# A feed-forward down product on one core: from a plain tiled product to a 2 by 2 Strassen block product

## The chip, the cores and the metric

The kernel runs on one core of one Trainium2 chip, as one program. The metric is the device time of one execution, in microseconds (us); lower is better. It is written engine by engine: TensorE (PE, the matrix products), VectorE (DVE), ScalarE (ACT) and GpSimd (POOL) each have their own list of instructions, SyncE (SP) issues all DMAs, and the lists meet only at counting semaphores. Each engine works its list in order: an instruction that waits holds up all behind it.

## The reference

Two decoder layers on x (2 x 512 x 1024). The change is in the last piece, the feed-forward of the second layer with low-rank (rank 16) additions to its weights:

```python
def _matmul_lora(x, w, a, b, scale=1.0):
    out = jnp.einsum('bsd,hd->bsh', x, w)
    out = out + jnp.einsum('bsr,hr->bsh', jnp.einsum('bsd,rd->bsr', x, a), b) * scale
    return out
gate = _matmul_lora(x, gate_w, gate_a, gate_b)
up = _matmul_lora(x, up_w, up_a, up_b)
hidden = jax.nn.silu(gate) * up                           # 1024 x 2752
out = _matmul_lora(hidden, down_w, down_a, down_b)        # 1024 x 1024
```

and the layer's output is x + out.

## The kernel before

Every large product is made of float16 pairs: an operand is split into a high part and a low part (value minus high part), and three matmuls of 128 x 128 weights by 512 columns (high x high, high x low, low x high) stand for one product. Making a pair takes ACT (the high part, a copy) and then DVE (the low part, a subtraction).

**Up and gate, "the slabs".** HID = 2752 hidden units are 21 slabs of 128 (j = 0 to 20) and a tail of 64 (TAIL = 21). For each slab, gate and up together are a 2 by 2 block product after Strassen: seven products of 12 matmuls in place of eight. The weight blocks are named A11, A12, S1, S2, S4, S3, A22; `form` (line 1674) makes the sums S1 to S4 on DVE, `block_hi` (987) and `block_lo` (1688) split them into a ring of 12 blocks. Low-rank parts are folded into the weights first: PE makes a rank-16 product (`fold`, 2462), and DVE adds it to the loaded weights (`slab_add`, 1666). What the products give is put together by DVE in `gate_second` (1700, waits for product S4), `up_second` (1706, waits for S3; product A22 of the same slab waits for it), `hidden_second` (1711), `hidden_first` (1717) and `hidden_rest` (1723), which leave the slab's hidden values as a pair in HIDT. The order of DVE's work is written out by hand at the end of the vector program, that of PE in `products` (92). SP loads a gate and an up slab of 512 KB per j (line 547), each as soon as the staging buffer of the one two slabs earlier is free.

**Down.** For each of 8 tiles of 128 output features (m) and both halves b of the 1024 rows, `down` (2554) sums over the 22 hidden tiles: 21 x 3 + 2 matmuls of 512 columns (the tail of 64 needs two), 65 x 16 = 1040 in all. The weights of the next m come in four pieces: `down_fold` (2542), `down_add` (1752), `down_hi` (1052), `down_lo` (1762), while PE works on the current m; their 1024 or 640 columns lie in two PSUM buffers in turn, and the outputs of m and m + 1 in two others. `finish` (1783) adds the scaled sum to the residual, which `residual_hi`, `residual_lo`, a transposing DMA (line 584) and `residual_sum` (1774) have brought in transposed form while the first m are worked on; `send` (503) writes it out. A hidden tile is used straight from HIDT.

Of the kernel before, what the change touches and what calls it, by code (L numbers as in the profile page):

```python
# [52 lines left out]
N_LOADS = N_DOWN + KD * NP  # L53
ZEROED = 8 + N_DOWN - N_DF
# [37 lines left out]
def products(j):  # L92
# [7 lines left out]
         + [(TAIL, "L3"), (TAIL, "L4")])  # L100
# [45 lines left out]
def build(nc, x, ctx, ctx_t, consts, small_w, w_branch, wq, wk, bqk, gate_w, up_w, tail_w,  # L146
          down_w, down_tail, gate_a, gate_bt, up_a, up_bt, down_a, down_bt, out_t, x_keep):
    stack = ExitStack()
    with stack:
# [50 lines left out]
        DWN = [SLAB[:, at * KB:at * KB + 2 * HT * P].rearrange("p (s k c) -> p s k c", s=2, k=HT) for at in (0, 13)]  # L200
        XR = XT[:, :, :, :, :].rearrange("p b s k t -> p (b s k t)").rearrange("p (g s d) -> p g s d", g=NT, s=2)
# [5 lines left out]
        XD = X[:, :, :].rearrange("p g d -> p (g d)").bitcast(F16).rearrange("p (s m t) -> p s m t", m=KD, s=2)  # L207
# [54 lines left out]
        DA, DB = LORA[:, D:D + HID], LORA[:, 0:D]  # L262
# [8 lines left out]
        def factors_of(g, si, sj):  # L271
# [26 lines left out]
        out_done, spilled, xd_ok = [sem("out_even"), sem("out_odd")], sem("spilled"), sem("xd_ok")  # L298
# [14 lines left out]
        fac_ok, s_add, comb, b_lo, d_add, d_lo, xr_lo, out_v = (  # L313
            sem(n) for n in ("fac_ok", "s_add", "comb", "b_lo", "d_add", "d_lo", "xr_lo", "out_v"))
# [11 lines left out]
        b_hi, sg_ok, hid_hi, p1_ok, p5_ok, p6_ok, d_hi, xr_hi = (  # L326
            sem(n) for n in ("b_hi", "sg_ok", "hid_hi", "p1_ok", "p5_ok", "p6_ok", "d_hi", "xr_hi"))
# [8 lines left out]
        fold_p, mul_p, dfold_p, down_p = (sem(n) for n in ("fold_p", "mul_p", "dfold_p", "down_p"))  # L336
# [17 lines left out]
            + [(("fold", n), s_add, n + 1) for n in range(BT, NS)]  # L354
            + [(("dfold", m, i), d_add, m * NP + i + 1) for m in range(KD) for i in range(NP)]))

# [81 lines left out]
        def block_source(j, name):  # L438


            st = [STAGE[(N_SLAB + 2 * j + i) % SLOTS].rearrange("p (h k c) -> p h k c", h=2, k=KD // 2)
                  for i in range(2)]
            a11, a12, a21, a22 = (st[i][:, h] for i in range(2) for h in range(2))
            if j == TAIL:
                return {"K1": (a11, 0, None, NS), "K2": (a12, 1, None, NS)}[name]
            s1 = ST[:, :].rearrange("p (k c) -> p k c", k=KD // 2)
            return {"A11": (a11, 0, None, 2 * j + 1), "A12": (a12, 1, None, 2 * j + 1), "A22": (a22, 1, None, 2 * j + 2),
                    "A21": (a21, 0, None, 2 * j + 2), "S1": (s1, 0, 1, 4 * j + 1), "S2": (s1, 0, 1, 4 * j + 2),
                    "S4": (a12, 0, 1, 4 * j + 3), "S3": (a21, 0, 1, 4 * j + 4)}[name]

        def down_pair(m):
            return PAIR[m % 2]
# [4 lines left out]
        def _(e):  # L457
# [45 lines left out]
            def send(m):  # L503
                for h in range(B):
                    hs = slice(h * HALF, (h + 1) * HALF)
                    e.wait_ge(out_v, B * m + h + 1)
                    e.dma_start(out_t[m * P:(m + 1) * P, hs], OUT[:, m % 2, hs]).then_inc(out_done[m % 2], 16)
# [31 lines left out]
            for n in range(NS):  # L539
# [4 lines left out]
                j, w_ = n // 2, up_w if n % 2 else gate_w  # L544
                at = N_SLAB + n
# [10 lines left out]
                elif n == SLOTS + 1:  # L556
                    for t in range(2):
                        for group in range(3):
                            turn_pieces(t, group)
                    for group in range(3):  # L560
                        for t in range(2, BT):
                            turn_pieces(t, group)
            factor(N_DF, down_bt)
            factor(N_DF + 1, down_a)
            for m in range(KD):
                for i, (k0, k1) in enumerate(PIECES):
                    at, p_ = N_DOWN + m * NP + i, m * NP + i
                    if p_ < SLOTS:
                        e.wait_ge(fac_ok, 8 + 4 + p_ - SLOTS + 1)
                    else:  # L570
                        e.wait_ge(d_lo, p_ - SLOTS + 1)
                    kp = HTAIL if k1 == HT else P
                    st = STAGE[at % SLOTS][0:kp, 0:(k1 - k0) * P].rearrange("p (k c) -> p k c", k=k1 - k0)
                    e.dma_start(st, down_tail[m] if k1 == HT else down_w[m][:, k0:k1, :]).then_inc(
                        stg_in[at % SLOTS], 16)
                if m == 0:
                    e.wait_ge(mul_p, len(ORDER))
                    e.wait_ge(spilled, 16 * BT)
                    for g in range(BT):
                        e.dma_start(X[:, g, :], x_keep[g * P:(g + 1) * P, :]).then_inc(x_in[g], 16)  # L580
                if m in (1, 2):
                    e.wait_ge(xr_lo, NT)
                    for g in range((m - 1) * BT, m * BT):
                        e.dma_start_transpose(XD.rearrange("p s m t -> p (s m) t")[:, :, g * P:(g + 1) * P],
                                              XR[:, g, :, :].rearrange("p s d -> p (s d)")).then_inc(x_in[g], 16)
                if m >= 2:
                    send(m - 2)
            send(KD - 2)
            send(KD - 1)
            for n in range(2):  # L590
                e.wait_ge(out_done[n], 16 * B * KD // 2)

        @prog.gpsimd
        def _(e):
# [130 lines left out]
            for b_, used in ((1, DONE[TAIL - 1, "S2"]), (0, len(ORDER))):  # L725
                e.wait_ge(mul_p, used)
                e.wait_ge(zero_ok, ZEROED + 1 - b_)
                e.memset(DWN[b_][P - HTAIL:P, 1, TAIL, :], 0.0).then_inc(zero_ok, 1)

        @prog.scalar  # L730
        def _(e):
# [255 lines left out]
            def block_hi(j, name):  # L987

                q = ready(j, name) - 1
                src, half, made, value = block_source(j, name)  # L990
                e.wait_ge(s_add if made is None else comb, value)
                if q < RING:
                    e.wait_ge(sc_p, NT)
                else:
                    e.wait_ge(mul_p, DONE[(q - RING) // NB, BLOCKS[(q - RING) % NB]])
# [38 lines left out]
            def tail_gate(b):  # L1034
# [16 lines left out]

            def down_hi(m, i):
                k0, k1 = PIECES[i]
                p_, kp = m * NP + i, HTAIL if k1 == HT else P
                at = N_DOWN + p_
                st = STAGE[at % SLOTS][0:kp, 0:(k1 - k0) * P].rearrange("p (k c) -> p k c", k=k1 - k0)
                e.wait_ge(d_add, p_ + 1)
                if m == 0:
                    e.wait_ge(mul_p, DONE[TAIL - 1, "S2"])
                elif m == 1:  # L1060
                    e.wait_ge(mul_p, len(ORDER))
                else:
                    e.wait_ge(down_p, 2 * (m - 1))
                last = e.activation(DWN[(m + 1) % 2][0:kp, 0, k0:k1, :], st, ACT.Copy)  # L1064
                if k1 == HT:
                    last = e.activation(DWN[(m + 1) % 2][P - kp:P, 0, k0:k1, :], st, ACT.Copy)
                last.then_inc(d_hi, 1)

            def residual_hi(g):
                e.wait_ge(mul_p, len(ORDER))  # L1070
                if g < BT:
                    e.wait_ge(x_in[g], TURNED + 16)
                else:
                    e.wait_ge(x3_ok, g + 1)
                e.activation(XR[:, g, 0, :], X[:, g, :], ACT.Copy).then_inc(xr_hi, 1)

# [217 lines left out]
            for j in range(TAIL):  # L1294
# [1502 lines left out]
```

## Time and profile before

| what | value |
|---|---|
| median of 3 runs | 1168.9 us (1167.17 to 1169.38) |
| the profiled execution, its own time | 1169.75 us |
| its span in the profile | 1167.9 us |
| PE busy, share of the span | 1103.2 us, 94% |
| DVE busy | 797.3 us, 68% |
| ACT busy | 484.6 us, 41% |
| slabs in the trace (products of j = 0 to 20 and the tail) | about 503 to 929 us |
| down product in the trace | 929 to 1165 us |

All times below are read from the profiled execution, in us from the start of its span; its own time is 0.85 us above the median. The start time of a matmul row says when it began; matmuls are pipelined, so the next may begin before the one before has ended. L numbers are lines of the kernel.

### The profile page before, as it was taken

How to read it: one execution, taken by the hardware profiler on the slowest of the kernel's cores; microseconds unless marked ns; L12 is line 12 of the kernel's file. 1: busy time of each engine (PE TensorE's matmuls, PEld its weight loads, DVE VectorE, ACT ScalarE, POOL GpSimd, SP SyncE). 2: the span in 40 equal slices, each digit the busy share in tenths (PEclk: the TensorE clock that was granted, in tenths of full speed). 3: DMA queues.
4: the chain of work that ended last, by engine and by line, in shares of the span. 5: the costliest groups of instructions: out<-in, count | busy, mean ns of one | idle time of the engine just before them, and what ended most of it. 6: DMA issues, size and time to landing. Idle time of an engine off the chain costs nothing.

```text
span 1167.9 us, 16025 instructions
## 1 busy us (share of the span) xinstructions
PE 1103.2 (94%) x6144; PEld 540.9 (46%) x6150; DVE 797.3 (68%) x1600; ACT 484.6 (41%) x731; POOL 154.2 (13%) x184
## 2 busy tenths in 40 slices
PE   4786999899999999969999999999999999999998
PEld 2343554654445444424444444444444444444443
DVE  8999988889994177877767676767766664333330
ACT  6896652873145134744343434434343341111110
POOL 4883350073004010000000000000001000000000
PEclk9997999999999999999999999999999999999999
DMA  9620000223032029864111212020111375322200
GB/s 367 270 97 1 2 1 1 73 69 112 1 108 86 1 60 248 194 131 93 71 57 53 72 38 72 37 73 36 73 37 39 89 198 120 111 66 68 65 14 25
DMA packets 80061, 97.19 MB, mean 83 GB/s; under 512 B 57776, under 2 KB 58416, under 8 KB 79984
## 3 DMA queue, kind: packets, MB, share of 16 engines
q1 hardware_dynamic: 79984, 96.16, 27.0%
q8 instruction: 49, 0.80, 0.3%
q14 instruction: 28, 0.23, 0.1%
HBM read 76.22 MB, written 6.29 MB: 71 GB/s over the span
## 4 chain that ended last, share of the span: by engine, by line
PE 76%; DVE 18%; ACT 3%; issue 2%; DMA 1%; SPq 0%; DVEq 0%; ACTq 0%
PE PAIR L2518 32%; PE PAIR L2170 13%; PE PAIR L2171 12%; PE PAIR L2172 12%; DVE X L1558 2%; DVE PAIR L1510 2%; PE PAIR L2473 2%; DVE LORA L1509 1%; DVE LORA L1511 1%; DVE POOL L1384 1%; PE PAIR L2550 1%; DVE BST L1356 1%; DVE BST L1357 1%; DVE X L1427 1%; DVE XT L1421 1%
## 5 line engine op out<-in xcount | busy, mean ns | idle before, releaser
L2170 PE MATMUL PAIR<-POOL 128*128 128x512 f16 x672 | 255.8, 381 | 2.3 <-DVE POOL L1601 2.3
L2171 PE MATMUL PAIR<-POOL 128*128 128x512 f16 x672 | 255.8, 381 | 0.0
L2172 PE MATMUL PAIR<-POOL 128*128 128x512 f16 x672 | 255.7, 381 | 0.0
L2518 PE MATMUL PAIR<-XT,POOL 128*128 128x512 f16 x1008 | 230.2, 382 | 10.6 <-DMA XT<-POOL 6.9
L2518 PEld LDWEIGHTS PAIR<-XT,POOL 128*128 128x128 f16 x1008 | 98.2, 98 | 127.1 <-issue 14.0
L2518 PE MATMUL PAIR<-X,POOL 128*128 128x512 f16 x504 | 115.7, 379 | 0.4 <-DMA X<-POOL 0.4
L2172 PEld LDWEIGHTS PAIR<-POOL 128*128 128x128 f16 x672 | 65.8, 98 | 80.3 <-issue 1.4
L2170 PEld LDWEIGHTS PAIR<-POOL 128*128 128x128 f16 x672 | 65.6, 98 | 69.3 <-DVE POOL L1601 4.3
L2171 PEld LDWEIGHTS PAIR<-POOL 128*128 128x128 f16 x672 | 65.7, 98 | 65.5 <-issue 0.6
L1064 ACT ACTIVATE POOL<-STG 128x1024 f16<-128x1024 f32 (+2 forms) x32 | 25.3, 790 | 169.7 <-DVE STG L1759 169.7
L1759 DVE SCALAR_TENSOR_TENSOR STG<-STG,PAIR 128x1024 f32<-128x1024 f32 (+2 forms) x32 | 28.3, 884 | 89.8 <-PE PAIR L2550 86.7
L667 POOL MEMSET STG<- 96x1024 f32 (+1 forms) x12 | 11.0, 923 | 522.5 <-DVE POOL L1691 475.7
L2518 PEld LDWEIGHTS PAIR<-X,POOL 128*128 128x128 f16 x504 | 48.4, 98 | 55.9 <-issue 1.1
L1691 DVE TENSOR_TENSOR POOL<-STG,POOL 128x512 f16<-128x512 f32 x107 | 69.7, 684 | 0.7 <-ACT POOL L996 0.7
L996 ACT ACTIVATE POOL<-STG 128x512 f16<-128x512 f32 x107 | 62.0, 621 | 3.7 <-DVE STG L1671 3.6
L1704 DVE TENSOR_TENSOR POOL<-POOL,PAIR 128x512 f32<-128x512 f32 x21 | 14.4, 688 | 71.4 <-PE PAIR L2518 71.4
L996 ACT ACTIVATE POOL<-ST 128x512 f16<-128x512 f32 x42 | 26.3, 626 | 80.6 <-DVE ST L1686 80.6
L2518 PE MATMUL PAIR<-T4B,POOL 128*128 128x512 f16 x252 | 57.8, 379 | 1.2 <-issue 1.2
L1671 DVE SCALAR_TENSOR_TENSOR STG<-STG,PAIR 128x1024 f32<-128x1024 f32 x43 | 52.1, 1214 | 0.0
L1510 DVE RECIPROCAL PAIR<-LORA 128x16 f32<-128x16 f32 (+1 forms) x168 | 46.8, 279 | 5.8
L2170 PE MATMUL PAIR<-XT,POOL 128*128 128x512 f16 x128 | 48.5, 379 | 1.2 <-ACT XT L906 1.2
L2172 PE MATMUL PAIR<-XT,POOL 128*128 128x512 f16 x128 | 48.5, 379 | 0.0
(305 smaller groups left out, 1707.9 us busy)
## 6 DMA issues: line engine op xcount, KB each, us to landing
STG<-in_gate_w SPq DMA_DIRECT2D x21, 512.0 KB, 3.5
STG<-in_up_w SPq DMA_DIRECT2D x21, 512.0 KB, 4.3
STG<-in_ctx_t SPq DMA_DIRECT2D x16, 512.0 KB, 3.8
STG<-in_ctx SPq DMA_DIRECT2D x16, 512.0 KB, 4.2
STG<-in_down_w SPq DMA_DIRECT2D x16, 512.0 KB, 3.6
POOL<-in_ctx SPq DMA_DIRECT2D x12, 512.0 KB, 11.1
X<-in_x SPq DMA_DIRECT2D x8, 512.0 KB, 9.7
out_t<-T4B SPq DMA_DIRECT2D x16, 256.0 KB, 2.0
```

The lines of the kernel that those rows point to most:

```text
L996: e.activation(block(j, name)[:, 0, :, :], src, ACT.Copy).then_inc(b_hi, 1)
L1064: last = e.activation(DWN[(m + 1) % 2][0:kp, 0, k0:k1, :], st, ACT.Copy)
L1510: chain(e.reciprocal(rr, rs))
L1558: i = e.scalar_tensor_tensor(xs, H[:, g, sj * CST:(sj + 1) * CST], factors_of(g, si, sj), xs, ALU.mult, ALU.add)
L1671: e.scalar_tensor_tensor(st, st, WS, PAIR[aux.pair("fold", n)][:, :], ALU.mult, ALU.add).then_inc(s_add, 1)
L1691: e.tensor_tensor(blk[:, 1, :, :], block_source(j, name)[0], blk[:, 0, :, :], ALU.subtract).then_inc(b_lo, 1)
L1759: e.scalar_tensor_tensor(st, st, WS, PAIR[aux.pair("dfold", m, i)][0:kp, 0:w_], ALU.mult, ALU.add).then_inc(d_add, 1)
L2170: e.matmul(dst, l_hi, r_hi, start=first, stop=False)
L2171: e.matmul(dst, l_hi, r_lo, start=False, stop=False)
L2172: return e.matmul(dst, l_lo, r_hi, start=False, stop=last)
L2473: i = e.matmul(PAIR[pr][:, k * P + c0:k * P + c0 + w], fa[0:GRP * 32, k * P:(k + 1) * P], fb[0:GRP * 32, j * P:j * P + w], start=True, sto ...
L2518: i = e.matmul(dst, blk[:, a_, k, :], src[:, b_, k, :], start=(opens and k == 0 and n == 0), stop=(k == KD // 2 - 1 and n == 2), skip_grou ...
```

## The change

The down product becomes a 2 by 2 block product after Strassen, like gate and up: output tiles in pairs (p = 0 to 3), rows in two halves, hidden tiles in 11 pairs (22 tiles, the tail padded with zeros). Each p is worked in three sets of 4, 4 and 3 tile pairs ("chunks", 12 in all), and a chunk is seven products of 3 matmuls per tile pair: 12 x 4, 12 x 4 and 9 matmuls a product, 7 x 33 x 4 = 924 in all.

```python
SETS = ((0, 4), (4, 8), (8, HT // 2))
NSET = len(SETS)
CHUNKS = NSET * KD // 2
```

**PE.** Each of the seven products of a p has a PSUM bank of its own for all three chunks, and one half bank (`bank_f`) takes the low-rank products, four for each chunk. So a low-rank product waits until DVE has added the one before it, and the first chunk of the next p writes the banks that hold the results of the last:

```python
bank_d = {"A11": PAIR[2][:, 0:HALF], "A12": PAIR[2][:, HALF:D], "S1": PAIR[3][:, 0:HALF], "S2": PAIR[0][:, 0:HALF],
          "S4": PAIR[0][:, HALF:D], "S3": bank_c, "A22": bank_b}
bank_f = PAIR[3][:, HALF:D]

def down_fold(j, i):
    d = j - HT
    e.wait_ge(s_add, NS + 4 * d + i)
...
for j in range(HT, HT + CHUNKS):
    first = 3 if j == HT else 0
    for n, name in enumerate(BLOCKS):
        down_product(j, name)
        if j + 1 < HT + CHUNKS and first <= n < first + 4:
            down_fold(j + 1, n - first)
```

`down_product` waits for its weight block, and in the first chunk of p = 1 to 3 for the bank: A11 for `first_ok` of the p before, A12, S1, S2, S4, S3, A22 for 1, 4, 3, 5, 8 and 13 of its 13 steps `acc_v`. For p = 0 it waits for the hidden values and the differences read back from DRAM.

**DVE and ACT, down.** Per chunk DVE makes four sums `down_add` (each of half the columns of a staged tile), four `form` and seven `block_lo`; ACT makes seven `block_hi`. Behind the last chunk of a p (`evacuate`, 13 steps on DVE, one `first_product` on ACT) the seven products are put together with the residual:

```python
def evacuate(p):
    o11, o12, o21, o22 = (out_part(a_, b_) for a_ in range(2) for b_ in range(2))
    j, at = HT + NSET * p + NSET - 1, ACCS * p
...
    e.wait_ge(sum_v, 2 * p + 1)
    scaled(o11, "A12", o11)
    e.wait_ge(first_ok, p + 1)
    e.wait_ge(acc_v, at + 1)
    added(o11, o21)
...
    e.wait_ge(acc_v, at + 12)
    scaled(o21, "A22", o21)
...
for d in range(1, CHUNKS + 1):
    if d < CHUNKS:
        j = HT + d
        down_add(j, 0)
        down_add(j, 1)
        block_lo(j, "A11")
        down_add(j, 2)
        down_add(j, 3)
        form(j, "S1")
...
        for name in ("S2", "S4", "S3", "A22"):
            block_lo(j, name)
    if d % NSET == NSET - 1:
        residual_sum(d // NSET, 0)
        residual_sum(d // NSET, 1)
    elif d % NSET == 0:
        evacuate(d // NSET - 1)
```

**The input's differences.** For each pair of hidden tiles three differences of half rows are needed as pairs. They are made in the slab loop, for a pair (j - 1, j) of slabs: on DVE `turn_first` or `turn_last` (one operation each) behind `hidden_first`, `turn_middle` (two) behind `hidden_second` of an odd j, `turn_lo` (two ahead of `gate_second`, one ahead of `up_second` of an even j), and on ACT three `turn_hi`. Eight of the eleven sets go to DRAM (`park`, 768 KB each) and come back at the end of the slabs (`back_in`).

**The residual** is now split, transposed and kept in DRAM within the slab loop: eight times (j = 2, 3, 4, 5, 7, 9, 11, 13) a `residual_hi` on ACT, a `residual_lo` on DVE ahead of `gate_second`, a transposing DMA ahead of the gate slab's load, and writes:

```python
                j, w_ = n // 2, up_w if n % 2 else gate_w
+               if n % 2 == 0 and j - 2 in R_AT:
+                   turn_residual(R_AT[j - 2])
                at = N_SLAB + n
...
+               if n % 2 and j - 2 in R_AT:
+                   keep_residual(R_AT[j - 2])
+               if n % 2 and 4 <= j and j % 2 == 0 and j // 2 - 2 < PARKED:
+                   park(j // 2 - 2)
```

`turn_residual(i)` waits for the i-th `residual_lo`. In the down stage it is read back by `load_sum` (4 x 256 KB for each p), whose last two reads stand ahead of the next p's first weights on SP:

```python
for p in range(KD // 2):
    load_sum(p, 0)
    load_sum(p, 1)
    for d in range(NSET * p + 2, min(NSET * p + 5, CHUNKS)):
        load_down(2 * d)
        load_down(2 * d + 1)
        if d == NSET * p + 2:
            load_sum(p, 2)
            load_sum(p, 3)
    send(p)
```

`load_sum(p, 2)` and `(p, 3)` wait for the two `residual_sum` of p.

**DVE at the end of a p, in the new order** (L1978 is `down_add`, L1865 `form`, L1870 `block_lo`, L2001 and L2004 `evacuate`; the first rows end the blocks of chunk 3, the first of p = 1):

```order
L1865 TENSOR_TENSOR STG<-STG,ST 128x512
L1865 TENSOR_TENSOR STG<-STG 128x512
L1870 TENSOR_TENSOR POOL<-ST,POOL 128x512
L1870 TENSOR_TENSOR POOL<-STG,POOL 128x512 x3
L2001 SCALAR_TENSOR_TENSOR T4B<-PAIR,T4B 128x512
L2004 TENSOR_TENSOR T4B<-T4B 128x512
L2001 SCALAR_TENSOR_TENSOR T4B<-PAIR,T4B 128x512 x3
L2004 TENSOR_TENSOR T4B<-T4B 128x512
L2001 SCALAR_TENSOR_TENSOR T4B<-PAIR,T4B 128x512 x2
L2004 TENSOR_TENSOR T4B<-T4B,LORA 128x512 x4
L2001 SCALAR_TENSOR_TENSOR T4B<-PAIR,T4B 128x512
L1978 SCALAR_TENSOR_TENSOR STG<-STG,PAIR 128x512 x2
```

The 13 steps of `evacuate` (L2001 and L2004) stand between the blocks of chunk 3 and the first sum of chunk 4 (the last row). Before, the only operations of the end of an m were one `residual_sum` and two `finish`, and PE waited for them not in the next m, but in the one after it.

**PE at the same place, in the new order** (L2892 is `down_product`, L2826 `down_fold`; the rows are the last products of chunk 2 and the first three of chunk 3):

```order
L2892 MATMUL PAIR<-POOL 128x512 x9
L2892 MATMUL PAIR<-X,POOL 128x512 x15
L2892 MATMUL PAIR<-LORA,POOL 128x512 x3
L2892 MATMUL PAIR<-POOL 128x512 x12
L2826 MATMUL PAIR<-LORA 128x128 x4
L2892 MATMUL PAIR<-POOL 128x512 x12
L2826 MATMUL PAIR<-LORA 128x128 x4
L2892 MATMUL PAIR<-POOL 128x512 x12
```

The row before the last is the second low-rank product of chunk 4; it waits for the first `down_add` of chunk 4 on DVE, and all products behind it wait with it.

**SP in the slabs, in the new order** (L592 is the transposing DMA of the residual, L676 a slab's load, L598 and L603 the writes to DRAM; before, this list held the two loads of each slab alone):

```order
L592 DMA_TRANSPOSE POOL<-POOL 128x16x128
L676 DMA STG<-in_gate_w 128x1024
L676 DMA STG<-in_up_w 128x1024
L598 DMA xt_keep<-POOL 128x8x128 x2
L592 DMA_TRANSPOSE POOL<-POOL 128x16x128
L676 DMA STG<-in_gate_w 128x1024
```

The load of slab j + 2 has moved behind a transposition that waits for DVE's `residual_lo` of slab j, and it is DVE's `slab_add` later in the same slab that uses it.

## Rows read from the trace of the kernel before

**Rows 1.** The page: busy time of PE, share of the span.

```profile
PE 1103.2 (94%) x6144; PEld 540.9 (46%) x6150; DVE 797.3 (68%) x1600; ACT 484.6 (41%) x731; POOL 154.2 (13%) x184
```

**Rows 2.** Windows: stretch, PE, PEld, DVE, ACT, POOL busy, granted clock, DMA share, GB/s.

```profile
600.00:900.00 300.00, 300.00 (x1583) 143.49 (x1581) 209.40 (x315) 122.56 (x207) 2.79 (x3) 1.00 0.15 53
930.00:1164.00 234.00, 234.00 (x1196) 109.85 (x1195) 82.48 (x95) 34.56 (x48) 0.00 (x0) 1.00 0.31 87
```

**Rows 3.** Timeline of PE, one slab period: start, length, engine, line, operation.

```profile
714.24 2.75 PE L2518 MATMUL PAIR<-XT,POOL 128*128 128x512 f16 x12
716.83 0.61 PE L2473 MATMUL PAIR<-LORA 96*128 96x128 f16 x8
717.28 2.76 PE L2518 MATMUL PAIR<-X,POOL 128*128 128x512 f16 x12
...
730.68 2.75 PE L2518 MATMUL PAIR<-T4B,POOL 128*128 128x512 f16 x12
733.27 2.75 PE L2518 MATMUL PAIR<-XT,POOL 128*128 128x512 f16 x12
```

**Rows 4.** Timeline of DVE, the same period; in brackets idle before and its releaser.

```profile
714.61 0.69 DVE L1721 SCALAR_TENSOR_TENSOR PAIR<-PAIR,POOL 128x512 f32<-128x512 f32 x1
715.21 0.68 DVE L1686 TENSOR_TENSOR ST<-ST,STG 128x512 f32<-128x512 f32 x1
715.92 0.69 DVE L1686 TENSOR_TENSOR STG<-STG,ST 128x512 f32<-128x512 f32 x1
...
723.11 0.69 DVE L1704 TENSOR_TENSOR POOL<-POOL,PAIR 128x512 f32<-128x512 f32 x1 [3.49 <-PE PAIR L2518]
...
724.92 1.21 DVE L1671 SCALAR_TENSOR_TENSOR STG<-STG,PAIR 128x1024 f32<-128x1024 f32 x1
728.29 0.69 DVE L1709 TENSOR_TENSOR POOL<-POOL,PAIR 128x512 f32<-128x512 f32 x1 [2.16 <-PE PAIR L2518]
```

**Rows 5.** Timeline of ACT, the same period: a high part.

```profile
718.05 0.62 ACT L996 ACTIVATE POOL<-STG 128x512 f16<-128x512 f32 x1
```

**Rows 6.** Timeline of PE: the last wait of the slabs, the first matmul of down.

```profile
920.60 0.61 PE L2550 MATMUL PAIR<-LORA 96*128 96x128 f16 x8 [0.78 <-DVE LORA L1663]
...
929.27 0.38 PE L2170 MATMUL PAIR<-POOL 128*128 128x512 f16 x1
```

**Rows 7.** Timeline of DVE: the last `finish`.

```profile
1164.75 0.69 DVE L1789 SCALAR_TENSOR_TENSOR T4B<-PAIR,T4B 128x512 f32<-128x512 f32 x1 [13.27 <-PE PAIR L2575]
```

**Rows 8.** Timeline of DVE: eight residual differences of 1024 columns.

```profile
938.52 9.17 DVE L1772 TENSOR_TENSOR XT<-X,XT 128x1024 f16<-128x1024 f32 x8 [0.80 <-ACT XT L1075]
```

**Rows 9.** Timeline of SP: a transposing DMA; time to issue.

```profile
497.57 1.47 SPq L501 DMA_TRANSPOSE X<-POOL  x1
...
511.45 2.48 SPq L501 DMA_TRANSPOSE X<-POOL  x1
```

**Rows 10.** Line L547, all loads of slabs: issue to landing.

```profile
DMA to landing us min/median/max: 3.3/4.1/6.2
```

**Rows 11.** The same line, 485 to 500: two loads right behind four transposing DMAs.

```profile
DMA to landing us min/median/max: 4.6/4.7/4.9
```

**Rows 12.** Line L574, 985 to 995: weights behind two DMAs of 256 KB.

```profile
DMA to landing us min/median/max: 5.1/6.0/6.3
```

**Rows 13.** Timeline of PE: idle stretches in brackets, and matmuls behind them.

```profile
109.31 0.38 PE L2170 MATMUL PAIR<-XT 128*128 128x512 f16 x1 [2.26 <-DVE XT L1545]
...
110.71 0.62 PE L2171 MATMUL PAIR<-POOL 128*128 128x512 f16 x1
...
515.28 2.75 PE L2518 MATMUL PAIR<-XT,POOL 128*128 128x512 f16 x12 [3.74 <-DVE POOL L1698]
...
525.79 5.08 PE L2518 MATMUL PAIR<-XT,POOL 128*128 128x512 f16 x12 [6.87 <-DMA XT<-POOL]
```

**Rows 14.** Windows around them, columns as in group 2.

```profile
110.00:115.00 5.00, 5.00 (x40) 2.36 (x39) 4.52 (x14) 5.00 (x10) 2.14 (x3) 0.66 0.00 0
...
525.00:530.00 5.00, 4.21 (x10) 1.50 (x11) 4.87 (x9) 1.24 (x2) 0.00 (x0) 0.50 1.02 191
```

More of the change, by code:

```diff
@@ new lines, in load_sum @@
+            def load_sum(p, i):
+                a_, b_ = ((0, 0), (0, 1), (1, 1), (1, 0))[i]
+                if i >= 2:
+                    e.wait_ge(sum_v, 2 * p + i - 1)
+                elif p:
+                    e.wait_ge(acc_v, ACCS * (p - 1) + (10, 12)[i])
+                else:
+                    e.wait_ge(t_lo, 3 * (HT // 2))
+                    for n in range(2):
+                        e.wait_ge(r_kept[n], LANDED + 16 * len(RESIDUAL))
+                e.dma_start(residual(i), xt_keep[2 * p + a_, :, :, b_ * HALF:(b_ + 1) * HALF]).then_inc(res_in[i % 2], 16)
@@ L593, in _ @@
+            for n in range(2):
+                e.wait_ge(out_done[n], 16 * KD)
         @prog.gpsimd
@@ new lines, in residual_hi @@
+            def residual_hi(i):
+                g = RESIDUAL[i][1]
+                if i >= 2:
+                    e.wait_ge(r_turned[i % 2], LANDED + 16 * (i // 2))
+                if g < BT:
+                    e.wait_ge(r_in[i % 2], LANDED + 16 * (i // 2 - 1))
+                else:
+                    e.wait_ge(x3_ok, g + 1)
+                if i == 0:
+                    for t in range(BT):
+                        for group in range(3):
+                            wait_turned(e, t, group)
+                e.activation(RH[i % 2][:, 0:D], X[:, g, :] if g >= BT else RESX[i % 2], ACT.Copy).then_inc(r_hi, 1)
@@ L1028, in tail_keep, with first_product @@
+            def first_product(p):
+                e.wait_ge(mul_p, DONE[HT + NSET * p + NSET - 1, "A11"])
+                if p:
+                    e.wait_ge(out_done[1], 32 * p)
+                else:
+                    e.wait_ge(mul_p, DONE[TAIL - 1, "A22"])
+                e.activation(out_part(1, 0), bank_d["A11"], ACT.Copy, scale=1.0 / (HS * WS)).then_inc(first_ok, 1)
             def tail_keep():
@@ L2116, in _ @@
                     factor(N_DF, DB, 2, WS)
+                    factor(N_DF + 1, DA[:, 0:HID], 1, 1.0, 0, 1)
+                if j in R_AT:
+                    residual_lo(R_AT[j])
+                if j and j % 2 == 0:
+                    turn_lo(j // 2 - 1, HELD3)
+                    turn_lo(j // 2 - 1, HELD2)
                 gate_second(j)
@@ L2137, in _ @@
                         block_lo(j + 2, name)
-            down_add(0, 0)
+            down_add(HT, 0)
+            e.memset(DA[:, HID:HT * P], 0.0)
+            factor(N_DF + 1, DA[:, 0:HID], 1, 1.0, 2)
+            down_add(HT, 1)
+            block_lo(HT, "A11")
+            block_lo(HT, "A12")
             hidden_first(TAIL - 1)
-            down_lo(0, 0)
+            turn_first(TAIL - 1)
+            down_add(HT, 2)
             tail_hidden(0)
             hidden_rest(TAIL - 1)
-            down_add(0, 1)
@@ L2144, in _ @@
[L2144 to L2145 removed]
+            down_add(HT, 3)
+            form(HT, "S1")
+            block_lo(HT, "S1")
+            for name in ("S2", "S4", "S3"):
+                form(HT, name)
+            block_lo(HT, "S2")
+            block_lo(HT, "S4")
             tail_sum()
             tail_hidden(1)
[L2148 to L2154 removed]
@@ L2155, in _ @@
-            for i in range(NP):
-                down_add(1, i)
-                down_lo(1, i)
-            for m in range(KD):
-                if m != 1 and m < KD - 1:
-                    for i in range(NP):
-                        down_add(m + 1 if m else 2, i)
-                        down_lo(m + 1 if m else 2, i)
-                residual_sum(m)
-                finish(m)
+            tail_rest(0)
+            block_lo(HT, "S3")
+            block_lo(HT, "A22")
+            tail_turn(HELD3)
```

570 lines of the change are left out of this document (368 added, 202 removed).

## The prediction, made before the changed kernel ran

> **What bounds the kernel now.** I read the page first, then windows by stage, then the timelines of single engines. The page shows PE busy for 94% of the span [rows 1], so the question is where PE has slack and who stands just behind it. The windows answer that: from 600 to 900 (the slabs) and from 930 to 1164 (down) PE is busy for every microsecond at full clock [rows 2]. Fewer matmuls there are worth their full time, unless another engine comes late. In the slabs DVE is at 70% (209.4 of 300), in down at 35% (82.5 of 234) [rows 2]. What matters is when it is idle: in a slab period of 19.03 us it waits 3.49 us for product S4 and 2.16 us for S3 [rows 3, 4].
>
> Prices from these rows. Twelve products of 512 columns take 2.59 us (714.24 to 716.83), 0.216 each; eight low-rank products take 0.45, 0.056 each [rows 3]. A half-width DVE operation takes 0.69 until its result is seen; the next begins after 0.60, or after 0.71 if it needs that result (715.21 to 715.92) [rows 4]. A high part on ACT takes 0.62 [rows 5], 0.66 with the hand-over.
>
> **What PE gains.** Before, down runs from 929.27 to the last `finish` at 1164.75 [rows 6, 7]: 235.5 us. Now 924 x 0.216 = 199.4, and of the 176 low-rank products 160 lie in it, 9.0; together 208.4, a gain of 27.1. The 0.78 us that PE waited for the last low-rank factor [rows 6] goes too, since the first low-rank product now needs only the first two pieces: 0.8. At the end something is given back. Before, one operation of 0.69 follows the last matmul. Now seven steps of `evacuate` depend on product S3, 7 x 0.71 = 5.0, and product A22 behind it (nine matmuls, 1.9) covers part: 3.1, so 2.4 more. **Net 25.5.**
>
> **What PE loses: the end of a p.** This is the largest cost. There is one half bank for low-rank products, so the second one of a chunk waits for DVE's first sum of that chunk, and after the last chunk of a p DVE does all 13 steps of `evacuate` before that sum. I count from when the fourth low-rank product of chunk 3 is seen, in the middle of chunk 2. DVE: sum 0.71, S1 0.71, high part on ACT 0.66, low part 0.71, S2 0.71, then S4, S3 and four low parts at 0.60: 7.1. `evacuate`: nine steps wait for the one before (0.71), four don't (0.60): 8.8. The first sum of chunk 4: 0.69. Together 16.6. PE: three products of nine matmuls 5.8, A11 2.59, a low-rank product 0.23, A12 2.59: 11.2, less 0.17, because a matmul's result comes that much after the next has begun (0.38 long, 0.21 apart). PE waits 5.6 us, partly at A11 for `first_product`, mostly at the low-rank product. This happens at three p ends: **16.8** (13.8 if all steps run at 0.60, 19.8 if each end costs 1 us more).
>
> **The start of down.** The low-rank products of chunk 1 lie behind the last four products of chunk 0, so the blocks of chunk 1 are late: from the fourth one DVE needs 7.1 + 0.69 = 7.8 to the first sum of chunk 2, PE only A11, a low-rank product and A12, 5.2. PE waits 2.6. One chunk earlier DVE has 28 operations between the second sum of chunk 0 (about 921.8) and the first of chunk 1, most at 0.60 to 0.71 and a few behind ACT, so I put that sum's result at 943.4; PE wants it at 941.6 and waits 1.8. **4.4** (2 to 8).
>
> **The weights of the next p.** SP issues them behind two `load_sum`, which wait for `residual_sum`. From the fourth low-rank product of chunk 2: blocks of 384 columns (0.56 each, estimated from 0.69 at 512 and 1.21 at 1024 columns [rows 4]) 5.8, two residual sums 1.3, issue 0.4, landing L, sum 0.69. PE: three products of 12, two of 9 and a low-rank one, 11.7. So the wait is L less 3.5. L was 3.3 at the least in the slabs [rows 10], 4.7 behind four transpositions [rows 11] and 6.0 behind two DMAs of 256 KB [rows 12]; reads may go better than those writes, so I take 4.7: 1.2 each, **3.6** (0 to 7.5).
>
> **The slabs.** The differences of the input are seven half-width operations for two slabs, 4.2 us against 2 x 5.65 idle; three high parts on ACT lie in its idle time. I cost them at nothing; if that cover were gone, they would cost 4.2 x 11 = 46. Writes to DRAM run between loads, and the next load is a period away. The residual is different: the gate load of slab j + 2 now stands behind a transposition that waits for `residual_lo`. Before, DVE was free from 719.6 (723.11 less 3.49) [rows 4]. For an odd j add `turn_first` 0.7 and the residual 1.15 (9.17 / 8) [rows 8]: 721.5. For an even j also two `turn_middle`: 722.7. Then issuing the transposition, 1.5 to 2.5 [rows 9], landing 4.6 to 4.9 [rows 11], `slab_add` 1.2, for an even j a `turn_lo` 0.6, `up_second` 0.69. Product A22 wants that at 730.68 [rows 3]. Odd j gives 729.5 to 730.8: 0 to 0.1. Even j gives 731.3 to 732.6: 0.6 to 1.9, and there are two (2 and 4). **2.5** (0 to 4.5). What is late behind it (`hidden_rest`, the next A11) has over 4 us in hand.
>
> **The clock.** Before, PE stood still for 2.26 us with thin work behind it and then ran at half rate (0.62 for a matmul, granted clock 0.66 over that stretch); 3.74 us left it at full rate; after 6.87 us twelve products took 5.08 in place of 2.59 [rows 13], at a granted 0.50, the lower of the two levels, 1.2 GHz [rows 14]. The new waits of about 4.7 at one place lie between. A fall costs 2.5 by the last case, some 1.7 by the first. Two of three fell, so I take 1.3 for each p end, **4.0** (0 to 7.5). The Trainium skill, "TensorE: Matmul & The Clock Gate", section "HAM oscillation — how this bites in real kernels", has it that waits between groups of matmuls throttle PE again each time, so that every group starts cold; it speaks against this change. The 6.87 us wait agrees, the 3.74 us wait shows no fall. By that rule all three ends would pay, about 6.3 in place of 4.0.
>
> **Sum.** -25.5 + 16.8 + 4.4 + 3.6 + 2.5 + 4.0 = +5.8. The profiled execution's own time is 1169.75, so 1175.5; it stands 0.85 above the median, and against that I say **1175 us**, slower.
>
> **The rivals.**
> - *The waits stay, the clock does not fall.* All as above without the 4.0: 1171, give or take 3. For it: 3.74 us did no harm. Against it: the fall behind 2.26.
> - *Faster: DVE is early enough.* One mechanism decides: how long DVE's chain from a chunk's fourth low-rank product to the next chunk's first sum is. Below 11 us PE never waits for it. If it runs nearer to that (steps at 0.60, weights landing at 3.3, chunk 1 in time), the waits come to about 16 in place of 24.8, and with no fall and no delay in the slabs the time is 1168.9 - 25.5 + 16 = 1160 (1155 to 1166). For it: DVE at 35% in down. Against it: the order of DVE's list and the 0.71 of steps that wait on each other.
> - *The slabs break.* If the transposition and the scattered writes before it delay the load at all eight residuals by 2 us more, each costs A22 that much: +16, 1191 (1184 to 1195). For it: only 0.1 us of room at an odd j. Against it: the queue is nearly empty there (DMA share 0.15 [rows 2]).
> - *The change does not do what it says*: the new order holds 924 products in down, so this has no weight.
>
> **The numbers.** Forecast (1171 to 1180) 0.47, clock stays 0.22, faster 0.18, slabs break 0.13. About 0.2%, 2.3 us, is what a measurement of this kernel can tell from no change: faster means below 1166.6, slower above 1171.2. Faster: the third case nearly whole, 0.18. Same: half of the second, the edge of the forecast and of the third, 0.22. Slower: 0.60. The range leaves out a part of the third case and most of the last: 1163 to 1184.
>
> **What would show it.** Right: PE idle in the slabs near two A22 only; in down, three waits of PE on `down_add` of 4 to 5 us with `evacuate` running, each behind a shorter one at A11, smaller ones before chunks 1 and 2 and on weights before each new p; last matmul to end of `evacuate` about 3 us; half clock behind some of the waits. Wrong: PE busy without gaps from 930 on (then the time is near 1145), waits in the slabs at all residuals, or a wait on a bank (`acc_v`) rather than on the sum.

## The result, and the profile after the change

The changed kernel took **1195.99 us** (median of 4 runs, 1192.45 to 1201.96) against 1169.14 us before on the same chip (4 runs): a ratio of 1.024, 95% interval 1.019 to 1.029, slower. The forecast was 1175 us, with a range of 1163 to 1184. The direction was right, the size wrong.

The profiled execution took 1193.59 us, its span is 1191.8. The page: busy time of each engine, as in [rows 1].

```profile
PE 1092.9 (92%) x6028; PEld 534.9 (45%) x6034; DVE 916.4 (77%) x1830; ACT 525.2 (44%) x815; POOL 155.7 (13%) x183
```

PE has 116 matmuls fewer, but it is busy only 10 us less, where the missing products alone are worth over 25: some of the remaining ones ran slower. And its share fell from 94% to 92%: it waits. The view of PE's waits from 540 on says for what (line that waits, releaser, us in total, times, longest). In the changed kernel L2826 is `down_fold`, L2794 a slab's product, L2892 `down_product`, L1978 `down_add`, L1888 `up_second`, L1870 `block_lo`.

```profile
PE PAIR L2826 <- DVE STG L1978: 27.2, 9, 4.8
PE PAIR L2794 <- DVE POOL L1888: 5.8, 4, 2.7
PE PAIR L2892 <- DVE POOL L1870: 2.8, 3, 0.9
```

That is 35.8 us in 16 waits; the kernel before had, from the product compared below on, only the 0.78 us of [rows 6]. Windows of the changed kernel, columns as in [rows 2]:

```profile
560.00:700.00 140.00, 134.21 (x697) 63.40 (x696) 115.02 (x172) 64.68 (x109) 0.00 (x0) 0.99 0.42 121
700.00:900.00 200.00, 200.00 (x1061) 95.75 (x1060) 166.58 (x251) 90.67 (x156) 0.95 (x1) 1.00 0.30 94
950.00:955.00 5.00, 4.48 (x16) 1.85 (x17) 1.76 (x3) 1.26 (x2) 0.00 (x0) 0.66 0.67 223
...
1010.00:1012.00 2.00, 2.00 (x6) 0.65 (x5) 0.22 (x1) 0.28 (x1) 0.00 (x0) 0.50 0.80 266
...
1050.00:1055.00 5.00, 5.00 (x21) 2.10 (x20) 1.98 (x3) 0.93 (x2) 0.00 (x0) 0.67 0.24 97
```

From 700 to 900 PE is full although DVE has gone from 70% to 83%: the differences of the input cost nothing there. From 560 to 700 (the slabs with residual pieces) 5.8 us are missing. In down there are stretches at a mean granted clock of 0.66 and 0.67, that is, with the lower level, 1.2 GHz, in part of them; from 1010 to 1012, behind the first end of a p, the granted clock is 0.50, that level throughout.

**The end of a p.** Timeline of DVE (L2001 and L2004 are `evacuate`), then of PE, changed kernel, start and length first:

```profile
998.34 0.68 DVE L2001 SCALAR_TENSOR_TENSOR T4B<-PAIR,T4B 128x512 f32<-128x512 f32 x1
...
1006.87 0.69 DVE L2001 SCALAR_TENSOR_TENSOR T4B<-PAIR,T4B 128x512 f32<-128x512 f32 x1
1007.48 0.68 DVE L1978 SCALAR_TENSOR_TENSOR STG<-STG,PAIR 128x512 f32<-128x512 f32 x1
```

```profile
990.67 0.39 PE L2826 MATMUL PAIR<-LORA 96*128 96x128 f16 x4
...
997.83 2.75 PE L2892 MATMUL PAIR<-POOL 128*128 128x512 f16 x12 [0.94 <-DVE POOL L1870]
1000.41 0.39 PE L2826 MATMUL PAIR<-LORA 96*128 96x128 f16 x4
1000.64 2.75 PE L2892 MATMUL PAIR<-POOL 128*128 128x512 f16 x12
1008.21 0.61 PE L2826 MATMUL PAIR<-LORA 96*128 96x128 f16 x4 [4.82 <-DVE STG L1978]
1008.61 4.58 PE L2892 MATMUL PAIR<-POOL 128*128 128x512 f16 x12
```

The first sum of chunk 4 starts behind the last step of `evacuate`, and PE's second low-rank product right behind that sum: 0.94 + 4.82 = 5.76 us of waiting, where the forecast had 5.6. What it had too small stands in the last row: the twelve products behind took 4.58 us, not 2.75. The two other ends read the same (0.94 and 4.82, then 4.44 us; 0.95 and 4.81, then 4.61).

**The weights of the next p.** SP, then DVE, then PE, changed kernel:

```profile
978.57 1.19 SPq L627 DMA_DIRECT2D LORA<-xt_keep  x2
979.79 2.02 SPq L613 DMA_DIRECT2D STG<-in_down_w  x4
...
985.57 0.69 DVE L1978 SCALAR_TENSOR_TENSOR STG<-STG,PAIR 128x512 f32<-128x512 f32 x1 [6.43 <-DMA STG<-in_down_w]
...
986.32 0.40 PE L2826 MATMUL PAIR<-LORA 96*128 96x128 f16 x4 [2.43 <-DVE STG L1978]
```

Two reads of the residual go first; the weights land 985.57 - 979.79 = 5.8 us after their issue began. PE waits 2.43, at the two other ends 2.75 and 2.58.

**The slabs.** SP, DVE and PE in slab 2, changed kernel (L592 is the transposition, L676 the loads, L1850 `slab_add`):

```profile
569.02 1.32 SPq L592 DMA_TRANSPOSE POOL<-POOL  x1
570.39 1.30 SPq L676 DMA_DIRECT2D STG<-in_gate_w  x1
...
576.18 1.22 DVE L1850 SCALAR_TENSOR_TENSOR STG<-STG,PAIR 128x1024 f32<-128x1024 f32 x1 [4.23 <-DMA STG<-in_gate_w]
...
578.75 2.75 PE L2794 MATMUL PAIR<-T4B,POOL 128*128 128x512 f16 x12 [1.78 <-DVE POOL L1888]
...
620.29 4.16 PE L2794 MATMUL PAIR<-T4B,POOL 128*128 128x512 f16 x12 [2.66 <-DVE POOL L1888]
```

DVE waits for the gate weights at all eight residuals; at four of them A22 is late: 1.78 (j = 2), 0.50 (3), 2.66 (4, the last row), 0.86 (7). The longest of these waits has another origin than the one at j = 2. DVE and SP in slab 4 (L1983 is `residual_lo`, L1883 `gate_second`):

```profile
609.94 1.22 DVE L1983 TENSOR_TENSOR POOL<-X,POOL 128x1024 f16<-128x1024 f32 x1
612.28 0.68 DVE L1883 TENSOR_TENSOR POOL<-POOL,PAIR 128x512 f32<-128x512 f32 x1
...
613.05 1.14 SPq L676 DMA_DIRECT2D STG<-in_gate_w  x1
```

The load lands 4.65 us after its issue began (5.76 in slab 2), but `residual_lo`, ahead of the transposition, comes late: `gate_second` starts without a wait, where it waited 3.49 us in [rows 4]. DVE had stood 4.23 and 4.37 us waiting for gate weights in slabs 2 and 3, and the work put off there was still ahead of it in slab 4.

**The account.** From one and the same product of the slabs (540.38 before, 538.75 after) to the end of the span it was 627.5 us before and is 653.1: 25.5 longer. By terms, us:

| term | predicted | measured | from |
|---|---|---|---|
| ends of p | 16.8 | 17.3 | 3 x (0.94 + 4.82) |
| start of down | 4.4 | 5.0 | 2.15 + 2.54 + 0.31 |
| weights of the next p | 3.6 | 7.8 | 2.43 + 2.75 + 2.58 |
| slabs | 2.5 | 5.8 | four waits at A22 |
| clock | 4.0 | 11.8 | seven groups of products too long by 1.4 to 1.9 |
| pipeline emptied at each wait | in the rows above | 2.7 | 16 x 0.17, worked out |
| sum of losses | 31.3 | 50.4 | |

With the predicted gain of 25.5 the measured losses give +24.9; +25.5 was seen. So the gain must have come nearly in full, and the losses are the story.

### The profile page after: what moved, and what is told of

It is laid out like the page before. It is cut to its first block and busy times, and to the rows that moved or that the text cites. A ratio compares the mean times of both kernels' runs of the same rounds, so it can differ in the third digit from the quotient of the medians.

```text
span 1191.8 us, 16325 instructions
## 1 busy us (share of the span) xinstructions
PE 1092.9 (92%) x6028; PEld 534.9 (45%) x6034; DVE 916.4 (77%) x1830; ACT 525.2 (44%) x815; POOL 155.7 (13%) x183
## 5 line engine op out<-in xcount | busy, mean ns | idle before, releaser
L2794 PE MATMUL PAIR<-XT,POOL 128*128 128x512 f16 x1008 | 231.2, 383 | 8.9 <-DMA XT<-POOL 5.2
L2794 PEld LDWEIGHTS PAIR<-XT,POOL 128*128 128x128 f16 x1008 | 98.5, 99 | 126.4 <-issue 14.1
L1130 ACT ACTIVATE POOL<-STG 128x512 f16<-128x512 f32 (+1 forms) x167 | 96.4, 612 | 128.6 <-DVE STG L1978 91.7
L2892 PE MATMUL PAIR<-POOL 128*128 128x512 f16 x528 | 129.9, 399 | 2.8 <-DVE POOL L1870 2.8
L2446 PE MATMUL PAIR<-POOL 128*128 128x512 f16 x336 | 128.1, 381 | 1.7 <-DVE POOL L1780 1.6
L2447 PE MATMUL PAIR<-POOL 128*128 128x512 f16 x336 | 128.0, 381 | 0.0
L2448 PE MATMUL PAIR<-POOL 128*128 128x512 f16 x336 | 128.0, 381 | 0.0
L2794 PE MATMUL PAIR<-X,POOL 128*128 128x512 f16 x504 | 115.7, 379 | 1.1 <-DMA X<-POOL 1.1
L1870 DVE TENSOR_TENSOR POOL<-STG,POOL 128x512 f16<-128x512 f32 (+1 forms) x167 | 106.2, 669 | 1.2 <-ACT POOL L1130 1.1
L1130 ACT ACTIVATE POOL<-ST 128x512 f16<-128x512 f32 (+1 forms) x64 | 39.5, 617 | 149.4 <-DVE ST L1865 149.4
L1978 DVE SCALAR_TENSOR_TENSOR STG<-STG,PAIR 128x512 f32<-128x512 f32 (+1 forms) x48 | 30.8, 642 | 88.9 <-PE PAIR L2826 69.1
L2892 PEld LDWEIGHTS PAIR<-POOL 128*128 128x128 f16 x528 | 52.3, 102 | 64.5 <-issue 10.7
L1850 DVE SCALAR_TENSOR_TENSOR STG<-STG,PAIR 128x1024 f32<-128x1024 f32 x43 | 52.2, 1216 | 28.7 <-DMA STG<-in_gate_w 28.7
L2794 PEld LDWEIGHTS PAIR<-X,POOL 128*128 128x128 f16 x504 | 48.4, 98 | 56.3 <-issue 1.5
L2794 PE MATMUL PAIR<-T4B,POOL 128*128 128x512 f16 x252 | 59.2, 386 | 7.0 <-DVE POOL L1888 5.8
L2448 PEld LDWEIGHTS PAIR<-POOL 128*128 128x128 f16 x336 | 32.9, 98 | 40.4 <-issue 1.1
L2446 PE MATMUL PAIR<-XT,POOL 128*128 128x512 f16 x128 | 48.5, 379 | 1.2 <-ACT XT L1040 1.2
L2448 PE MATMUL PAIR<-XT,POOL 128*128 128x512 f16 x128 | 48.5, 379 | 0.0
L2447 PE MATMUL PAIR<-XT,POOL 128*128 128x512 f16 x128 | 48.5, 379 | 0.0
L2446 PEld LDWEIGHTS PAIR<-POOL 128*128 128x128 f16 x336 | 32.8, 98 | 32.4 <-DVE POOL L1780 3.9
```

The source lines that it names most:

```text
L1130: e.activation(block(j, name)[:, 0, :, :], src, ACT.Copy).then_inc(b_hi, 1)
L1850: e.scalar_tensor_tensor(st, st, WS, PAIR[aux.pair("fold", n)][:, :], ALU.mult, ALU.add).then_inc(s_add, 1)
L1870: e.tensor_tensor(blk[:, 1, :, :], block_source(j, name)[0], blk[:, 0, :, :], ALU.subtract).then_inc(b_lo, 1)
L1978: e.scalar_tensor_tensor(st, st, WS, bank_f[:, 0:depth(j) * P], ALU.mult, ALU.add).then_inc(s_add, 1)
L2446: e.matmul(dst, l_hi, r_hi, start=first, stop=False)
L2447: e.matmul(dst, l_hi, r_lo, start=False, stop=False)
```

## The experiments

Each kernel below is the changed one but for the edit shown. The times of before on the same chip were 1167.8 us beside the first four, 1167.2 beside e5 and e6 and 1167.6 beside e7 and e8; ratios are to those, with 95% intervals.

**e1: DVE's first sums between the pieces of `evacuate`.**

```diff
 # evacuate: yield behind the steps 3, 6, 8 and 13
+steps = evacuate(d // NSET - 1) if d > NSET and d % NSET == 1 else iter(())
+next(steps, None)
 down_add(j, 0)
+next(steps, None)
 down_add(j, 1)
 block_lo(j, "A11")
+next(steps, None)
 down_add(j, 2)
+next(steps, None)
 down_add(j, 3)
...
-elif d % NSET == 0:
-    evacuate(d // NSET - 1)
```

> Only the order of DVE's list is changed: the 13 steps of evacuate are split into pieces of 3, 3, 2 and 5 that stand between the four first sums of the next chunk, in place of wholly ahead of them. Theory (the half bank: PE's second low-rank product waits for a sum that stands behind evacuate, and each such wait of 4.8 us is followed by twelve products at half rate, 4.4 to 4.6 in place of 2.6): the three waits of 4.8 us on down_add go or fall under 1 us, the half-rate products behind them go too, so 3 x (4.8 + 1.9 + 0.2) = 21 us less: about 1175, 1171 to 1180. The waits of 0.94 at A11 stay, those on weights (2.4 to 2.75) too. Rival (the banks themselves are the limit: the products of the next p need evacuate's steps, wherever the sums stand): the same time is spent in waits on acc_v at S1, S3 or A22 in place of down_add, and the time stays at 1190 or above.

Measured: 1176.0 us, ratio 1.006 (1.004 to 1.008). PE's waits from 970 on in this kernel (L2835 is `down_fold`, L2901 `down_product`):

```profile
PE PAIR L2835 <- DVE STG L1978: 8.6, 3, 3.4
PE PAIR L2901 <- DVE POOL L1870: 2.8, 3, 0.9
```

The three waits of 4.8 are gone, and no bank took their place; left are the waits on weights and at A11. With the same half bank, the place of the sums alone cost 20 us of the 27, by the length of the waits and the slow products behind them together. The rival falls.

**e2: weights ahead of the last two reads of the residual.**

```diff
-if d == NSET * p + 2:
+if d == min(NSET * p + 3, CHUNKS - 1):
     load_sum(p, 2)
     load_sum(p, 3)
```

> Only SP's order is changed: the last two load_sum of a p stand behind the weight loads of the next p's first chunk. Theory (the weights are late because they stand behind two reads that wait for residual_sum): the three waits of 2.4, 2.75 and 2.6 us before the first chunk of p = 1 to 3 go, and with them the half-rate products behind two of them (1.6 and 1.7 us): 7.8 + 3.3 + 0.5 = 11.6 less, about 1184, 1181 to 1188. The waits of 4.8 at the ends stay. Rival (landing is slow by itself, 5.7 us after the issue, from the share of the other transfers): waits of about 2 us stay and the time changes by under 3 us.

Measured: 1184.2 us, ratio 1.013 (1.010 to 1.016). PE's waits from 970 on:

```profile
PE PAIR L2826 <- DVE STG L1978: 14.5, 3, 4.8
PE PAIR L2892 <- DVE POOL L1870: 2.8, 3, 0.9
```

Only the three ends are left. The weights were late by the place of two reads in SP's list, which held back their issue and also lengthened their landing: the weights of the first chunk of p = 1 are now issued at 965.17, and the view of L613 from 964 to 970 has them land sooner than the 5.8 to 8.1 us of the four loads in the changed kernel.

```profile
DMA to landing us min/median/max: 3.5/4.0/4.6
```

In the same trace the weights that now stand right behind the two reads take 6.3 to 6.7 us (the first load of each pair). So the rival, that landing is slow by itself, falls too.

**e3: the transposition behind the slab's two loads.**

```diff
-if n % 2 == 0 and j - 2 in R_AT:
-    turn_residual(R_AT[j - 2])
...
 if n % 2 and j - 2 in R_AT:
+    turn_residual(R_AT[j - 2])
     keep_residual(R_AT[j - 2])
```

> Only SP's order in the slabs is changed: the transposing DMA of the residual stands behind the gate and up load of its turn in place of ahead of them. Theory (the gate load is late behind the transposition): DVE's slab_add no longer waits for the load, the waits of 1.78, 0.50, 2.66 and 0.86 us at A22 go, and the half-rate products behind the third (1.4): 5.8 + 1.4 = 7.2 less, about 1188, 1186 to 1191. Rival (DVE's added differences make up_second late, not the load): A22 waits as before, time unchanged within 2 us.

Measured: 1188.2 us, ratio 1.016 (1.012 to 1.020). No wait of PE is left in the slabs. DVE's waits there, 540 to 920 (L1887 is `up_second`, L1882 `gate_second`):

```profile
DVE POOL L1887 <- PE PAIR L2793: 35.8, 20, 2.2
DVE POOL L1882 <- PE PAIR L2793: 20.9, 17, 2.8
```

DVE waits for PE only, as in [rows 4], and not for `in_gate_w`, on which it had waited 28.7 us. The added operations on DVE are covered; the order of SP's list was the cost.

**e4 and e7: PE kept busy during the 4.8 us.** e7 is e4 unchanged, run again beside the changed kernel (e8).

```diff
+if name == "A12" and j > HT and (j - HT) % NSET == 0:
+    e.wait_ge(acc_v, ACCS * ((j - HT) // NSET - 1) + 3)
+    for _ in range(20):
+        e.matmul(bank_d["S2"], HIDT[:, 0, 0, 0:P], HIDT[:, 0, 0, 0:HALF], start=True, stop=True)
```

> Only PE's list is changed: in the first chunk of p = 1 to 3, ahead of the low-rank product that waits 4.8 us, PE makes 20 products of 512 columns (4.3 us at full rate) that nobody uses, in a bank that the next product but two clears. Nothing is left out. The wait ends when it did, but PE isn't idle in it. Theory (the clock falls because PE stands still, and that costs by itself): no half-rate products behind the ends of p, 3 x 1.8 to 2.0 = 5.5 to 6 us less than the changed kernel, 1189 to 1191; the waits of 2.4 to 2.75 on weights and what follows them stay. Rival (half rate has another cause, or the wait alone costs): the twelve products behind the end still take 4.4 to 4.6 us and the time is that of the changed kernel, or more by what the extra products overrun the wait (0 to 1 us each).

> The kernel that keeps PE busy at the ends of p once more. Theory: the twelve products behind each of the three ends take 2.75 again in this trace, and the time stays 5 to 8 us below the changed kernel on the same chip (1188 to 1191 against 1196). Rival (its first trace was lucky, and the clock falls behind the ends whether PE works or not): half rate behind at least one of the three ends, and a time within 2 us of the changed kernel.

> The changed kernel once more, as it is, for a second trace and for times on the same chip as the kernel that keeps PE busy. Theory: 1196, 1192 to 1201; the waits are as long as before (4.8 at each end of a p, 2.2 to 3.6 before the first chunk of the next), all three ends are followed by half rate, the shorter waits only in part, so the spread between runs stays at some 10 us.

Measured: e4 1188.2 us, 1.018 (1.013 to 1.023); e7 1190.6, 1.019 (1.017 to 1.022); e8, the changed kernel, 1196.4, 1.025 (1.023 to 1.027). PE at the third end in e7 (L3065 are the products that nobody uses), then at the same end in e8:

```profile
1129.55 4.48 PE L3065 MATMUL PAIR<-POOL 128*128 128x512 f16 x20
1134.53 0.40 PE L2826 MATMUL PAIR<-LORA 96*128 96x128 f16 x4 [0.50 <-DVE STG L1978]
1134.77 2.76 PE L2892 MATMUL PAIR<-POOL 128*128 128x512 f16 x12
```

```profile
1135.51 0.60 PE L2826 MATMUL PAIR<-LORA 96*128 96x128 f16 x4 [4.82 <-DVE STG L1978]
1135.90 4.27 PE L2892 MATMUL PAIR<-POOL 128*128 128x512 f16 x12
```

The sum comes no earlier, but with PE at work until 0.5 us before it the twelve products take 2.76 us, at all three ends of both traces; in e8 they take 4.80, 4.44 and 4.27. The clock is a cost of its own beside the wait: 5.8 us between e7 and e8 on one chip. e4's profiled execution was the fastest of its four (1182.8), and none of its waits on weights was followed by slow products; the median is what counts.

**e5: the three orders together**, and `first_product` one place earlier on ACT.

```diff
 for name in BLOCKS:
+    if name == "S1" and d % NSET == 0:
+        first_product(d // NSET - 1)
...
-if d % NSET == 0:
-    first_product(d // NSET - 1)
```

> The three reorderings together (sums between the pieces of evacuate, weights ahead of load_sum, transposition behind the loads), and first_product earlier in ACT's list, ahead of the S1 high part of the last chunk of a p. Theory (each wait has its own cause, so the gains of 20, 12 and 8 us add up, and the three waits of 0.94 at A11 go too): 1196 - 40 - 2.8 = 1153, 1150 to 1158, below the kernel before. Of waits in down only those of the start stay (0.3, 2.15, 2.54). Rival (DVE is the bound of the end of a p: what one order saves the next wait takes): new waits of 1 to 3 us at the sums or on acc_v at each end, 1160 to 1166.

Measured: 1149.4 us, ratio 0.986 (0.984 to 0.988). The gains of e1, e2 and e3 (20, 12 and 8) add up, with some 7 us more: 2.8 for A11, the rest argued only, from the one slow group of products that this trace has left in down (last row). All that PE still waits for in down is at its start:

```profile
941.65 0.40 PE L2835 MATMUL PAIR<-LORA 96*128 96x128 f16 x4 [2.15 <-DVE STG L1978]
...
955.57 0.50 PE L2835 MATMUL PAIR<-LORA 96*128 96x128 f16 x3 [2.54 <-DVE STG L1978]
955.87 4.08 PE L2901 MATMUL PAIR<-POOL 128*128 128x512 f16 x12
```

**e6: the start of down eased too.**

```diff
+down_add(HT + 1, 0)        # ahead of the last two turn_lo
...
-first = 3 if j == HT else 0
+first = 3 if j == HT else 1 if j == HT + 1 else 0
```

> As the kernel with the three reorderings, and the start of down eased: the first sum of chunk 1 stands ahead of the last two turn_lo on DVE, and the low-rank products of chunk 2 begin one product later. Theory: the waits of 0.3, 2.15 and 2.54 before chunks 1 and 2 go or fall under 0.7, and the half-rate products that follow one of them (1.7): 4.5 to 6.5 us less than that kernel, 1147, 1143 to 1152. Rival (the chain of blocks on DVE at the start is the bound, and an earlier sum only makes the blocks behind it later): the waits move to products of chunk 0 or 1 (on the differences or on block_lo), time within 2 us of that kernel.

Measured: **1142.9 us**, ratio 0.979 (0.978 to 0.981): 2.1% faster than the kernel before, with the change's arithmetic untouched, only the order of the lists. PE's waits from 540 on, then two windows of down:

```profile
PE PAIR L2837 <- DVE STG L1978: 0.3, 1, 0.3
```

```profile
920.00:1000.00 80.00, 79.60 (x417) 37.52 (x414) 63.51 (x103) 26.67 (x46) 0.00 (x0) 1.00 0.45 156
1000.00:1130.00 130.00, 130.00 (x677) 61.94 (x676) 84.16 (x141) 29.17 (x52) 0.00 (x0) 1.00 0.24 81
```

And DVE at the first end of a p, where the sums now stand between the steps:

```profile
981.74 0.69 DVE L2001 SCALAR_TENSOR_TENSOR T4B<-PAIR,T4B 128x512 f32<-128x512 f32 x1
982.35 0.68 DVE L1978 SCALAR_TENSOR_TENSOR STG<-STG,PAIR 128x512 f32<-128x512 f32 x1
...
984.26 0.69 DVE L2004 TENSOR_TENSOR T4B<-T4B 128x512 f32<-128x512 f32 x1
984.87 0.68 DVE L1978 SCALAR_TENSOR_TENSOR STG<-STG,PAIR 128x512 f32<-128x512 f32 x1
```

## Why the prediction was wrong in size and right in direction

*What PE gains (25.5 net): right.* In e6, where nearly no wait is left, it is 1140.7 - 537.4 = 603.3 us from the product named above to the end, against 627.5 before: 24.2 gained, with 0.3 of waiting in it. The tail, in the changed kernel's timelines of PE and then DVE, is 1189.31 less 1186.09, the ends of these rows: 3.2 us, predicted 3.1.

```profile
1185.28 0.81 PE L2892 MATMUL PAIR<-LORA,POOL 128*128 128x512 f16 x3
...
1188.62 0.69 DVE L2001 SCALAR_TENSOR_TENSOR T4B<-PAIR,T4B 128x512 f32<-128x512 f32 x1
```

*The ends of a p (16.8): right*, 17.3, at the places named: a short wait at A11 for `first_product`, a long one on `down_add`. DVE's chain, counted at 16.6 us, took 17.1: from the low-rank product seen at 991.06 to the end of the first sum at 1008.16. e1 shows that the order of the sums is its cause.

*The start of down (4.4): nearly right*, 5.0.

*The weights of the next p (3.6): failed in the term L.* "Landing L less 3.5" gives 2.3 with the landing of 5.8, and 2.43 was waited. I had taken 4.7, with the ground that reads may go better than the writes of [rows 12]; 6.0, the row with two DMAs of 256 KB ahead, was the nearest case and would have given 7.5. A median of the case most like the new one should not be talked down without a row.

*The slabs (2.5): failed in size.* The mechanism held, with the even j the worst (1.78 and 2.66, against 0.6 to 1.9), but the odd ones weren't free (0.50 and 0.86, against 0.1 at most). Two steps failed. The landing, taken as 4.6 to 4.9 from [rows 11], was 5.76 at j = 2 and 6.35 at j = 7; at the six other residuals it was 4.3 to 4.7, and which transfer lengthens the two wasn't told apart. And every slab was counted as if DVE began it as early as in [rows 4]: that held for j = 2 and 7, but `residual_lo` ended 7.6 us before A22 wanted its operand at j = 3 and 6.3 before at j = 4, where the prediction has 9.2 and 8.0. The sentence that what is late behind `up_second` "has over 4 us in hand" asked only whether PE would wait for it, not when the next residual's transposition would start.

*The clock (4.0): failed, the largest miss, 7.8 us.* The prediction priced a fall only behind the three long waits, and there at two chances in three, from the three cases of [rows 13]. The clock fell behind all three, which cost 5.4; and it fell behind two of the three waits on weights, one of the two at the start of down, and one in the slabs, which cost 6.4 and had no term at all. These waits were in the sum (forecast at 0.6 to 2.6 us each, measured at 2.15 to 2.75), and the fall behind 2.26 us in [rows 13] stood beside them. The price of 2.5 for a fall sets the 5.08 us of the row against 2.59 from start to start; against the 2.75 of [rows 3] it is 2.3, and here it was 1.4 to 1.9. The rival "the clock does not fall" is out by the rows behind the ends of p, and by e4, e7 and e8.

*The pipeline (2.7)*: a wait in brackets begins when the last matmul is seen, 0.17 us after its successor could have begun, and the prediction counted its waits from that earlier moment. In its own terms the ends of a p came to 18.3 us, the start of down to 5.5, the weights to 8.3 and the slabs to 6.5.

*The rivals.* "DVE is early enough" is what e5 and e6 made true by order alone, with the same operations. "The slabs break" named the right place with too much: 5.8 us and one fall in place of 16. And the range was too narrow above, for its terms were taken as if independent: a late load in one slab left DVE late in the next, and each wait that came out longer brought its own chance of a fall of the clock.

## To carry to other kernels

Removing matmuls from a full PE is worth their full time only if each engine's list is looked through for what now stands ahead of PE's next operand: here three places in two lists, a burst of 13 steps, two reads and a transposition, cost 40 us and turned a gain into a loss of 27, and moving them, with no operation less, gave it back. Price each new standstill of PE as its length plus a chance of slower matmuls behind it, also where it is short. Where an engine is held up in one period, ask what it does late in the next. Take a transfer's landing from the stretch whose queue is most like the new one.

## What the runs showed that I had not expected

The clock doesn't follow from the length of a standstill alone. Counted over the ten traces, from 495 us on, standstills of PE of at least 1.5 us: behind none of 9 of 1.5 to 2.1 us were the next products slow; behind 15 of 31 of 2.14 to 3.12 us; behind all 7 of 3.28 to 3.54, 8 of 10 of 3.73 and 3.74, and all 22 of 3.9 and more. One and the same wait goes either way: 2.15 us at the start of down was followed by 4.44 us for twelve products in the changed kernel's trace and by 2.75 in e5's, and 2.54 us the other way round:

```profile
950.52 0.40 PE L2826 MATMUL PAIR<-LORA 96*128 96x128 f16 x4 [2.15 <-DVE STG L1978]
950.76 4.44 PE L2892 MATMUL PAIR<-X,POOL 128*128 128x512 f16 x12
...
966.14 0.34 PE L2826 MATMUL PAIR<-LORA 96*128 96x128 f16 x3 [2.54 <-DVE STG L1978]
966.32 2.75 PE L2892 MATMUL PAIR<-POOL 128*128 128x512 f16 x12
```

(changed kernel; e5's rows stand above). What decides it is open. The 3.74 us of [rows 13], which the prediction took as a wait that leaves the clock alone, is one and the same wait in all ten traces, and behind eight of them the products were slow: that row was luck, and one row is one sample. That a wait goes either way may also be why the changed kernel's times spread: 9.5 us from lowest to highest in its first 4 runs, 3.2 in the 4 of e6, which has no such waits in down; no run tests that by itself. The Trainium skill, "TensorE: Matmul & The Clock Gate", section "HAM oscillation — how this bites in real kernels", describes a kernel in which PE waits some 3 to 5 us between its groups of matmuls and is throttled again each time, and advises another order of the loop, in which it keeps its full clock. All the ends of p agree with the first (4.8 us each, twelve out of twelve in the traces of the changed kernel, its second run, e2 and e3), and of the waits of 2.14 to 3.12 us about half also lowered the clock; e6 agrees with the second (granted clock 1.00 in both windows above).
